# 42 in place of 28 blocks gathered during the coefficient stage, with GpSimd's graph-layer program written out

## What is computed

```
w_full = einsum('rb,bdo->rdo', w_comp, weight)        # 16 edge types out of 8 bases
msg    = einsum('nd,rdo->rno', feat, w_full)[etypes, src] * norm
out    = relu(segment_sum(msg, dst) + h_bias + feat @ loop_weight)
x      = x + out                                       # feat is the layer norm of x
x      = x + layer_norm(x' + top-2 of 16 experts(x'))  # x' is the layer norm of x
```

## Time and profile before

| | us |
|---|---|
| median of three runs | 2809.38 |
| the profiled execution | 2809.64 |
| its span | 2807.4 |
| TensorE matmuls busy | 2223.8 (79%) |
| GpSimd busy | 1810.5 (64%) |
| VectorE busy | 965.7 (34%) |
| ScalarE busy | 653.3 (23%) |
| mean granted TensorE clock | 0.912 |
| stage `expand`, from the start of the span | 84 to 157 |
| stage `graph_layer`, from the start of the span | 157 to 2205 |

### The profile page before, as it was taken

One profiled execution on the slowest core, in us unless ns is written; L12 is line 12 of the kernel. 1 busy time (PEld: TensorE's weight loads), 2 busy tenths in 40 slices (PEclk: granted clock), 3 DMA queues, 4 the chain that ended last, 5 costly groups with the idle time before them and its releaser, 6 DMA issues. The chain is left out here.

```text
span 2807.4 us, 44573 instructions
## 1 busy us (share of the span) xinstructions
PE 2223.8 (79%) x11549; PEld 1851.5 (66%) x11550; DVE 965.7 (34%) x2172; ACT 653.3 (23%) x1539; POOL 1810.5 (64%) x2000
## 2 busy tenths in 40 slices
PE   1779999999998888786776767567556579999987
PEld 0568787877777666665564646446444379999975
DVE  6743333242243322221321212112112543333347
ACT  2532323233222212111111010001000233233245
POOL 0557767777777777777777777777776035555544
PEclk9999999999999989998898878778877799999998
DMA  6544434444443434334333333333333642222246
GB/s 207 168 146 120 131 108 123 122 118 142 116 122 114 136 109 119 115 115 129 108 109 116 119 112 103 108 100 116 105 103 90 225 152 69 69 71 69 71 134 219
DMA packets 146325, 339.11 MB, mean 121 GB/s; under 512 B 36674, under 2 KB 56290, under 8 KB 146051
## 3 DMA queue, kind: packets, MB, share of 16 engines
q0 software_dynamic: 89296, 245.33, 29.9%
q1 hardware_dynamic: 39311, 59.54, 6.2%
q10 hardware_dynamic: 17588, 32.88, 3.6%
HBM read 292.84 MB, written 47.97 MB: 121 GB/s over the span
## 5 line engine op out<-in xcount | busy, mean ns | idle before, releaser
L1069 POOL DMA_INDIRECT rows<-feat,idx x1540 | 1464.3, 951 | 492.0 <-issue 432.2
L1278 PE MATMUL psW<-rows,S 128*128 x3920 | 1065.6, 434 | 379.0 <-SPq L1026 347.0
L1278 PEld LDWEIGHTS psW<-rows,S 128*128 128x128 f32 x3920 | 843.6, 220 | 596.7 <-issue 460.0
L1150 DVE TENSOR_TENSOR S<-psHere,coefS 128x896 f32<-128x896 f32 x280 | 301.2, 1090 | 1346.5 <-PE psW L1278 1338.4
L1338 ACT COPY z<-psW 128x512 f32<-128x512 f32 x196 | 114.7, 585 | 1427.4 <-PE psW L1278 1426.7
L1244 PE MATMUL psG<-wb,zT 128*128 128x256 f32 (+1 forms) x1600 | 353.5, 379 | 0.0
L1244 PEld LDWEIGHTS psG<-wb,zT 128*128 128x128 f32 (+1 forms) x1600 | 301.1, 188 | 44.2
L1729 PE MATMUL psH<-xT,w1x 128*128 128x128 f32 x1840 | 226.8, 277 | 0.2
L1680 POOL DMA_INDIRECT expert_rows<-os,at_rows x114 | 113.7, 997 | 171.8 <-DVE os L1788 171.8
L1729 PEld LDWEIGHTS psH<-xT,w1x 128*128 128x128 f32 x1840 | 216.4, 193 | 2.0 <-issue 1.9
L1738 PE MATMUL psO<-w2s,hT 128*128 x912 | 215.8, 380 | 0.0
(11 more groups left out here) (284 smaller groups left out, 1439.7 us busy)
## 6 DMA issues: line engine op xcount, KB each, us to landing
rows<-feat,idx POOLq DMA_INDIRECT x1568
g<-expert_rows SPq DMA_DIRECT2D x24, 512.0 KB, 5.1
w1s<-in_L_ffn_w SPq DMA_DIRECT2D x8, 1024.0 KB, 10.0
w2s<-in_L_ffn_w SPq DMA_DIRECT2D x16, 512.0 KB, 10.1
feat<-rows SPq DMA_DIRECT2D x24, 256.0 KB, 3.0
fts<-feat ACTq DMA_DIRECT2D x24, 256.0 KB, 2.9
h<-in_x ACTq DMA_DIRECT2D x24, 256.0 KB
y_rows<-y ACTq DMA_DIRECT2D x24, 256.0 KB
```

The costliest lines, as they stand in the source:

```text
L1069: e.indirect_dma_start(rows[:, at * H:(at + 1) * H], None, d.feat, bass.IndirectOffsetOnAxis(ap=idx[:, q * GB + u:q * GB + u + 1], axis=0) ...
L1150: e.tensor_tensor(S[h0 + h][:, :].rearrange("p (s b n) -> p s b n", s=U, b=B), both[:, h * U:(h + 1) * U, :].unsqueeze(2).to_broadcast([P, ...
L1278: last = e.matmul(psW[:, bass.ds(bank[u], H)], S[h][:, u * ZC:(u + 1) * ZC], rows[:, bass.ds(slot[u], H)], start=False, stop=True, skip_gr ...
```

## The change

`EG` becomes 3, so that 42 blocks are gathered in `expand`, three after each of the eight later edge gathers. The gathers take their row numbers from `srcT` itself, at addresses fixed when the program is made. For that, GpSimd's program of `graph_layer` has no loop any more: the other 1526 gathers are written out one after the other, each with its own constant wait on `s_in`. The buffer `idx`, its copies, the semaphores `s_list`, `s_pool` and `s_paced` go. The waits on `s_P` stay, from group 4 on, and so do the loads of `room`, eight words at group 3 and at each eighth group.

```diff
-EG = 2
+EG = 3
@@ expand, GpSimd
             def ahead(j):
                 if j >= AHEAD:
                     e.wait_ge(s_row[(j - AHEAD) % ROWS], 16 * ((j - AHEAD) // ROWS + 1))
-                e.indirect_dma_start(rows[:, j * H:(j + 1) * H], None, d.feat, bass.IndirectOffsetOnAxis(ap=idx[:, j:j + 1], axis=0)).then_inc(s_row[j % ROWS], 16)
+                e.indirect_dma_start(rows[:, j * H:(j + 1) * H], None, d.feat, bass.IndirectOffsetOnAxis(ap=srcT[:, j:j + 1], axis=0)).then_inc(s_row[j % ROWS], 16)
             for g in range(SG):
                 if g == GR:
                     e.iota(win_no[:, :], [[1, WPAD]], base=0, channel_multiplier=0, allow_small_or_imprecise_dtypes=True).then_inc(s_const, 1)
-                    for q in range(EG + 1):
-                        e.tensor_copy(idx[:, q * GB:(q + 1) * GB], srcT[:, q * GB:(q + 1) * GB]).then_inc(s_list, 1)
                     e.wait_ge(s_feat, 16 * NT2)
-                    e.wait_ge(s_list, EG + 1)
@@ graph_layer, GpSimd
-            ch = Chain(e, s_pool)
             regs, room_held = ([e.alloc_register(f"{n}{q}") for q in range(IB)] for n in ("room", "room_held"))
-            last = NBLK // (IB * GB) - 1
-            def list_in(group, q):
-                ch.add(e.tensor_copy(idx[:, q * GB:(q + 1) * GB], srcT[:, bass.ds(group * GB, GB)]))
-            def landed(i, n):
-                e.wait_ge(s_in, i * (IB * GB) + (n + 1))
-                e.sem_inc(s_paced, 1)
-            def blocks(i):
-                e.load(regs, room[0:1, bass.ds(i * IB, IB)])
-                free = at_least_one(e, regs, room_held)
-                for q in range(0 if later(i) else EG, IB):
-                    if later(i) or q >= RB // GB:
-                        e.wait_ge(s_P, free[q])
-                        e.sem_inc(s_turn, 1)
-                    if later(i) or q > EG:
-                        ch.wait()
-                    if q < IB - 1 or not isinstance(i, int) or i < last:
-                        list_in(i * IB + q + 1, (q + 1) % IB)
-                    else:
-                        e.sem_inc(s_turn, 1)
-                    for u in range(GB):
-                        at = (q * GB + u) % RB
-                        landed(i, q * GB + u - AHEAD)
-                        e.indirect_dma_start(rows[:, at * H:(at + 1) * H], None, d.feat, bass.IndirectOffsetOnAxis(ap=idx[:, q * GB + u:q * GB + u + 1], axis=0)).then_inc(s_row[at % ROWS], 16)
-            blocks(0)
-            with e.Fori(1, last) as i:
-                ch.base, ch.n = IB * i - EG, 0
-                blocks(i)
-            ch.base, ch.n = IB * last - EG, 0
-            blocks(last)
+            def blocks(group):
+                if group % IB == 0 or group == EG:
+                    i = group // IB
+                    e.load(regs, room[0:1, i * IB:(i + 1) * IB])
+                    at_least_one(e, regs, room_held)
+                if group >= RB // GB:
+                    e.wait_ge(s_P, room_held[group % IB])
+                    e.sem_inc(s_turn, 1)
+                for j in range(group * GB, (group + 1) * GB):
+                    e.wait_ge(s_in, j - AHEAD + 1)
+                    e.indirect_dma_start(rows[:, j % RB * H:(j % RB + 1) * H], None, d.feat, bass.IndirectOffsetOnAxis(ap=srcT[:, j:j + 1], axis=0)).then_inc(s_row[j % ROWS], 16)
+            for group in range(EG, NBLK // GB):
+                blocks(group)
```

More of the change, by code:

```diff
@@ L647, in _, with expand @@
                 src_columns(q)
-def expand(nc, d, wcd, halfs, win_n, ident, tables, wend, pairs, jcol, wcol, spread, dstS, wgtS, coefS, s_got, s_feat, srcT, idx, rows, s_row):
+def expand(nc, d, wcd, halfs, win_n, ident, tables, wend, pairs, jcol, wcol, spread, dstS, wgtS, coefS, s_got, s_feat, srcT, rows, s_row):
     from contextlib import ExitStack
@@ L699, in expand @@
         s_js, s_cz, s_ctl = sem("js"), sem("ctl_ready"), sem("ctl")
-        s_near, s_list = sem("near_st"), sem("lists")
+        s_near = sem("near_st")
         s_lst = [sem(f"late_st{k}") for k in range(DL)]
@@ L965, in _, with graph_layer @@
             e.tensor_scalar(ident[:, :], ident_i[:, :], 0.0, None, ALU.is_equal)
-def graph_layer(nc, d, a, ctl, pairs, room, wend, srcT, dstS, wgtS, coefS, ident, wb, lw, hb, gw, s_w, logit, choice, mean, rstd, idx, rows, s_row):
+def graph_layer(nc, d, a, ctl, pairs, room, wend, srcT, dstS, wgtS, coefS, ident, wb, lw, hb, gw, s_w, logit, choice, mean, rstd, rows, s_row):
     from contextlib import ExitStack
@@ L1002, in graph_layer @@
         s_in = sem("rows_in")
-        s_pool, s_turn, s_paced, s_zr, s_node = sem("pool"), sem("pool_turn"), sem("pool_paced"), sem("zero"), sem("node")
+        s_turn, s_zr, s_node = sem("pool_turn"), sem("zero"), sem("node")
         s_late = [sem(f"late{k}") for k in range(len(CHUNK))]
@@ L1995, in gnn @@
         srcT = sb("srcT", [P, NBLK], I32)
-        idx = sb("idx", [P, IB * GB], I32)
         rows = sb("rows", [P, RB * H])
@@ L2013, in gnn @@
             coefS = sb("coefS", [P, NEAR * CS * B])
-            expand(nc, d, wcd, halfs, win_n, ident, tables, wend, pairs, jcol, wcol, spread, dstS, wgtS, coefS, got, s_feat, srcT, idx, rows, s_row)
+            expand(nc, d, wcd, halfs, win_n, ident, tables, wend, pairs, jcol, wcol, spread, dstS, wgtS, coefS, got, s_feat, srcT, rows, s_row)
         wb, lw, hb, gw = sb("wb", [P, HC, B, H]), sb("lw", [P, HC, H]), sb("hb", [P, H]), sb("gw", [P, HC, X])
-        graph_layer(nc, d, a, ctl, pairs, room, wend, srcT, dstS, wgtS, coefS, ident, wb, lw, hb, gw, s_w, logit, choice, mean, rstd, idx, rows, s_row)
+        graph_layer(nc, d, a, ctl, pairs, room, wend, srcT, dstS, wgtS, coefS, ident, wb, lw, hb, gw, s_w, logit, choice, mean, rstd, rows, s_row)
 def program(nc, a, out):
```

## The result

The changed kernel takes **2774.1 us** (median of four runs, 2771.3 to 2776.1) against 2809.0 for the kernel before (2807.9 to 2809.4). The ratio is 0.9876, with a 95% interval of 0.9859 to 0.9893: 34.8 us less. I had forecast 2787 us and a range of 2778 to 2798. The profiled execution took 2774.9 us, with a span of 2772.9 (before: 2809.6 and 2807.4).

The account below looks back on a forecast made before the run. TensorE was taken to bound graph_layer first, GpSimd later. Longer expand +9.3, low clock +1.3, quicker gather -0.6, jumps -23.0 and copies -9.3 sum to -22.3 us: 2787 us forecast, range 2778 to 2798.

Parts of the forecast that it names:

- The bound, and where it changes: In graph_layer, TensorE bounds the first phase, until about 894 us; from then on GpSimd does.
- Head start lost in the ring: 14 more gathers in expand, 17.5 us, gain nothing: the ring is full; GpSimd never waits for room after 514.5 us.
- A longer expand stage, +10.0: Later start of graph_layer +9.3 us, TensorE's low clock +1.3, quicker gather behind the ring's wait -0.6.
- Jumps, -23.0: GpSimd's loop in graph_layer: ten jumps back behind block 294, 1.5 to 3.5 us each, go when written out.
- Copies, -9.3: GpSimd in graph_layer: copies cost 0.10 us a group; over 90 groups behind block 294 the sum is -9.3 us.
- The register arithmetic and the counts on s_paced go too, at nothing: GpSimd in graph_layer: removing them saves 0 us, since expand has the same 0.30 us between gathers without them.
- gaps over 0.3 us at even distances: Sign that the forecast is wrong: such gaps in GpSimd's straight program after the change.
- C: Rival: the head start is kept, as TensorE isn't the first phase's bound; -56 us, 2754 us, chance 0.02.
- D: Rival: TensorE's phase reaches to about 1450 us, GpSimd's savings lost in the ring; 2808 us, chance 0.06 together with E.
- F: Rival: GpSimd stalls fetching its written-out program, 14 x 2.3 = 32 us; slower, 2819 us, chance 0.05.
- A: Rival: cheap drain after expand, next stage 3.1 us behind the last gather; -28.4 us, 2781 us, chance 0.13.
- E: Rival: each of GpSimd's 14 loads of room stalls it 1.6 us; about 2809 us, chance 0.06 together with D.

Follow-up runs that it names:

- s_eg2: The changed kernel with EG = 2 in place of 3, so 28 blocks gathered ahead: 2764.4 us, ratio 0.9837.
- s_eg1: The changed kernel with EG = 1 in place of 3, so 14 blocks gathered ahead: 2766.8 us, ratio 0.9839.
- l_eg3: The kernel before with EG = 3 alone, its loop, copies and counts kept: 2817.4 us, ratio 1.0029.
- u_all: The kernel before with its loop written out, copies, counts on s_paced and loads of room kept: 2789.3 us, ratio 0.9931.
- u_nopaced: u_all without the count on s_paced, so that the gather itself carries the wait: 2773.1 us, ratio 0.9877.
- s_paced: s_eg2 with a separate wait that counts on the semaphore s_paced ahead of each gather: 2781.3 us, ratio 0.9898.
- s_count: s_eg2 with a separate count on the semaphore s_paced behind each gather, the wait staying in the gather: 2766.6 us, ratio 0.9843.
- gb4_c: s_eg2 with room in the ring taken in steps of 4 blocks, not 14, on a chip like the first ones: 2764.3 us, ratio 0.9836.
- after_again: The changed kernel itself, run again on a chip where every kernel was a third slower: 3713.9 us, ratio 0.992.
- eg2_again: The changed kernel with EG = 2, run again on the chip where every kernel was a third slower: 3717.6 us, ratio 0.9931.
- s_gb4: s_eg2 with room taken in steps of 4 blocks, not 14, on the chip a third slower: 3644.8 us, ratio 0.9723.

## Why the prediction was right in direction and wrong in size

**The bound, and where it changes.** Right. TensorE's turns keep one distance (7.9 us late) until about 890 us, then come earlier and earlier: at the 130th turn 2 us early, at the 202nd 21, at the 274th 35. In the window from 1700 to 1900 us TensorE still waits for rows most of what it did:

```profile
PE psW L1255 <- SPq L1023: 66.5, 18, 5.4
```

**Head start lost in the ring.** Right in its effect: s_eg2, s_eg1 and l_eg3 show that 14 or 28 blocks ahead are worth nothing. Wrong in a detail, "after that GpSimd never waits for room". TensorE is 7.9 us later, GpSimd on its way from block 294 to 448 some 8 us quicker (193.9 us to the end of the gather ahead of it, where before takes 202.3 to block 448 with its jump), and at block 448 they meet once more: its group needs a turn behind a tile product, which ends at about 721. That gave 5.3 us back. I had checked the ring where GpSimd waits today, not where it would wait once it is quicker. The jump that stood at block 448 had covered this place.

**A longer expand stage, +10.0.** Measured +7.5 at block 294. The last gather ended where I said (159.2, forecast 159.7). The empty queue came 5.1 us behind it, not 6.5, in both kernels that have 42 blocks ahead; TensorE's turns came later by another 0.2 us at the first and 0.5 from the eleventh on, not 1.3: the zeroing ran at the lower level (634 ns for each matmul), but the first turn took 3.28 us as before. The 4.97 us of the earlier trace rows, which I took for a turn at the lower level, was only partly one; after's last turn shows 6.19. I had taken the upper bound of the drain, since its rows were of the same gathers; the truth lay between the bounds. The fit of the Trainium skill, "DMA: Bandwidth & Descriptors", section on the anatomy of a GpSimd DMA, gave a shift of 6.8 us by the prediction's estimate; the trace has 7.3, nearer to it than to my 9.3. The base is also less sharp than I treated it: the nine kernels with 28 blocks ahead (before among them, on chips where it takes 2809 to 2811 us) begin graph_layer anywhere from 153.7 to 157.7 us. Why they differ isn't shown; before's start, 156.9, lies near the late end, so the difference of two such starts can be off by 2 to 3 us.

**Jumps, -23.0.** Right in kind, too large. u_all measured -20.2, of which 17.5 lie behind block 294 by the trace. The jump blocks themselves gained 20.0: at block 448 a wait for room of 2.2 us stands where the jump was. The other 2.5 are small differences spread over the stage.

**Copies, -9.3.** Right in size: -8.7 by the times, -10.1 by the traces. But 1.0 of my 9.3 was the stall at block 883, which I had read as the price of a copy.

**"The register arithmetic and the counts on s_paced go too, at nothing".** This step failed, and with it the forecast. I argued from the usual gap of 0.30 us, which is the same in expand without them. The usual gap was the wrong row: the cost isn't in it but in 1.1 us once in 106 gathers, which no group's mean shows. The rows to read were there: in the waits of before, 58.3 us in 94 waits for SPq L1026, and a timeline of the second phase shows 1.5 us of them between two plain gathers. I had even written that "gaps over 0.3 us at even distances" would be a sign in the changed program, and never looked for them in the one before. What the runs show in place of the nothing is 15.5 to 16.2 us for the wait that stands alone (u_nopaced), 14.8 with the number of instructions kept (s_paced against s_count). With 14.4 us for the stalls (the one at block 883 is in the copies) and 5.3 for block 448 the sum would have been 2778; with the measured shift of the stage, 2776.

**The rivals.** Nothing of C, D or F was seen: no time for the head start, TensorE's phase ends where it did, and the written-out program has no gap over 0.3 us apart from waits. A was right in that the drain is shorter, and its 2781 was still too slow. E showed only in gb4_c. The Trainium skill's 200 ns a register ("Runtime: NRT & Kernel Launch", section on instruction fetch) would have made 1.6 us of each load of eight words. In the trace of after the sequencer takes 0.80 us for the first such load and 0.56 to 0.58 for the other 13, and none of those behind block 294 shows as a gap between gathers.

## What to carry to other kernels

Before a loop is costed, list **every** gap between like instructions that exceeds the usual one, and its distance from the last: means and "usual gap" rows hide a stall that comes once in a hundred. Keep the wait on the instruction that needs it; an instruction between the wait and the DMA, even one that takes no time, can cost 15 us over 1500 DMAs. A head start for an engine that fills a ring is worth nothing while the consumer is the bound, and what it lengthens is paid in full; smaller steps in taking room (6.1 us less by the traces, 4.8 by times whose intervals overlap) did more than more blocks ahead.

## What I had not expected of the hardware

GpSimd pauses once in 106 indirect gathers, for 3.1 us in its sequencer, of which 1.1 show in the time if its waits stand alone and none or up to 0.5 us if they are carried by the gathers. The pauses keep their distance from graph_layer's first gather, whatever else is issued between the gathers. Whether the pause is there in an execution that isn't recorded is not tested.

On two of the chips all kernels, the kernel before included, took 3645 to 3760 us. This is the timeline of TensorE there (after_again, in the middle of graph_layer), and its waits:

```profile
1839.29 1.19 PE L1255 MATMUL psW<-rows,S 128*128 x2 [0.21 <-issue]
1840.69 1.19 PE L1255 MATMUL psW<-rows,S 128*128 x2 [0.21 <-issue]
1857.49 1.19 PE L1255 MATMUL psW<-rows,S 128*128 x2 [15.61 <-issue]
```

```profile
POOL rows L1052 <- PE psW L1255: 767.2, 33, 37.1
...
PE psW L1255 <- issue: 500.0, 297, 15.6
```

TensorE stands up to 15.6 us in the middle of its turns with nothing to wait for, 500 us in all. In its sequencer's record the register instructions around such places take about 700 ns each, where they take about 55 on the other chips: 510 of 4481 in the whole trace. VectorE (149 of 2616) and SyncE (49 of 230) have such instructions of 700 ns too; ScalarE and GpSimd have none, and after on its first chip has none on any engine. GpSimd's gathers cost the same 948 ns and wait 767 us for room. The row waits of TensorE's turns are small beside that (39.7 us for SPq L1023), so TensorE is the bound over most of the stage. Between after_again and eg2_again no difference shows within their scatter (26 and 32 us from lowest to highest), and the step in which room is taken matters most (s_gb4 -2.8%). Why these two chips do this is open.
